# Memory attention on one core: the state update over three engines, logits and scores at other places in a step

## The reference, cut to what matters

```python
x = x + 0.5 * _L0_ffn_ref(_layernorm(x), gate_w, w1, w2)      # 8 experts, top 1
x = x + _L0_attn_ref(_layernorm(x), ...)
x = x + 0.5 * _L0_ffn_ref(_layernorm(x), gate_w, w1, w2)

def _mem_loss(p, k_t, v_t):                 # W1, W2 are 64 x 64
    pred = jax.nn.silu(k_t @ W1.T) @ W2.T
    return jnp.sum((pred - v_t) ** 2)

for c0 in range(0, S, CHUNK):               # CHUNK = 128: 8 chunks
    g = _grad_fn(W_state, k[:, sl], v[:, sl]) * GRAD_SCALE     # per token, norm clipped to 1
    # for each token t: S = eta_t * S - theta_t * g_t;  W = (1 - alpha_t) * W + S
    (S_state, W_state), Wtraj = jax.lax.scan(step, (S_state, W_state), xs)
    h = silu(einsum('btd,btod->bto', q[:, sl], W1t))
    outs.append(einsum('bto,btpo->btp', h, W2t))
out = retrieved @ Wo.T
out = out * rsqrt(mean(out * out, -1) + EPS) * norm_g
return out * (hidden @ gW.T + gb)
```

## Time and profile before

| | |
|---|---|
| median of 3 runs | 743.57 us (742.95 to 744.75) |
| profiled execution, its own time | 744.95 us |
| its span, first to last instruction | 743.1 us |
| busy in it: PE / PEld | 654.3 us (88%) / 574.0 us (77%) |
| busy: DVE / ACT / POOL | 570.0 (77%) / 430.5 (58%) / 249.9 us (34%) |
| attention, roughly | from 195 to 576 us of the span |
| granted TensorE clock, mean | 0.952 |

### The profile page before, as it was taken

One profiled execution on the slowest core, in us unless ns is written; L12 is line 12 of the kernel. 1 busy time (PEld: TensorE's weight loads), 2 busy tenths in 40 slices (PEclk: granted clock), 3 DMA queues, 4 the chain that ended last, 5 costly groups with the idle time before them and its releaser, 6 DMA issues. The chain is left out here.

```text
span 743.1 us, 15272 instructions
## 1 busy us (share of the span) xinstructions
PE 654.3 (88%) x5531; PEld 574.0 (77%) x5531; DVE 570.0 (77%) x1395; ACT 430.5 (58%) x1094; POOL 249.9 (34%) x206
## 2 busy tenths in 40 slices
PE   5538999999697899999999999999988389999995
PEld 2228889898576788989888898988866168999985
DVE  0878888773388989899898989988765878887851
ACT  1416485562355867687786777776643445667450
POOL 0033553123311536162452516243241061651302
PEclk9859999999799999999999999999999579999999
DMA  9959727160332104325141432504123624652401
GB/s 336 413 203 355 275 88 262 51 206 23 128 115 86 59 29 149 110 75 182 58 143 60 140 118 64 195 1 154 48 67 104 227 73 165 238 191 115 141 10 35
DMA packets 63586, 101.97 MB, mean 137 GB/s; under 512 B 8200, under 2 KB 50336, under 8 KB 63392
## 3 DMA queue, kind: packets, MB, share of 16 engines
q1 hardware_dynamic: 51536, 83.01, 32.5%
q0 software_dynamic: 3840, 10.49, 4.3%
q10 hardware_dynamic: 8144, 7.61, 3.3%
HBM read 87.31 MB, written 22.16 MB: 147 GB/s over the span
## 5 line engine op out<-in xcount | busy, mean ns | idle before, releaser
L726 PE MATMUL ps<-moe_normedT_high,weights_high_up 128*128 128x320 f32 x252 | 80.9, 321 | 0.6 <-DVE moe_hidden_low L544 0.5
L727 PE MATMUL ps<-moe_normedT_low,weights_high_up 128*128 128x320 f32 x252 | 78.2, 310 | 0.0
L728 PE MATMUL ps<-moe_normedT_high,weights_low_up 128*128 128x320 f32 x252 | 78.2, 310 | 0.0
L726 PE MATMUL ps<-weights_high_down,moe_hidden_high 128*128 128x256 f32 x256 | 73.5, 287 | 0.3 <-DVE weights_rows L552 0.3
L728 PE MATMUL ps<-weights_high_down,moe_hidden_low 128*128 128x256 f32 x256 | 71.6, 280 | 0.0
L727 PE MATMUL ps<-weights_low_down,moe_hidden_high 128*128 128x256 f32 x256 | 71.5, 279 | 0.0
L544 DVE SCALAR_TENSOR_TENSOR moe_hidden_low<-ps,moe_hidden_high 128x256 fp32r<-128x256 f32 x128 | 53.9, 421 | 22.7 <-ACT moe_hidden_high L681 18.5
L640 ACT CAST weights_high_down<-weights_raw_down 128x256 fp32r<-128x256 f32 x96 | 35.0, 406 | 39.8 <-PE ps L728 33.3
L1247 POOL TENSOR_TENSOR weights_raw_up<-weights_raw_up,att_AB 128x1024 f32<-128x1024 f32 x8 | 17.6, 2197 | 114.0 <-DVE att_ENDS L1457 114.0
L726 PEld LDWEIGHTS ps<-weights_high_down,moe_hidden_high 128*128 128x128 f32 x256 | 48.0, 188 | 3.7 <-issue 3.1
L318 DVE TENSOR_TENSOR weights_low_down<-weights_raw_down,weights_high_down 128x256 fp32r<-128x256 f32 x128 | 49.8, 416 | 0.0
(11 more groups left out here) (326 smaller groups left out, 2008.7 us busy)
## 6 DMA issues: line engine op xcount, KB each, us to landing
weights_raw_up<-in_w SPq DMA_DIRECT2D x16, 1024.0 KB, 7.8
weights_raw_down<-in_w SPq DMA_DIRECT2D x16, 1024.0 KB, 8.2
first_xt<-in_xT SPq DMA_DIRECT2D x8, 1024.0 KB, 8.0
weights_rows<-x SPq DMA_DIRECT2D x8, 1024.0 KB, 5.5
out_x<-weights_rows SPq DMA_DIRECT2D x8, 1024.0 KB, 4.5
weights_rows<-x ACTq DMA_DIRECT2D x7, 1024.0 KB, 5.5
att_AB<-decays_row SPq DMA_DIRECT2D x32, 129.0 KB, 2.9
att_eta<-rates_row SPq DMA_DIRECT2D x8, 512.0 KB, 3.9
```

Source lines behind the costliest of these rows:

```text
L726: mm(dst, high_l, high_r, start=start, stop=False)
L727: mm(dst, high_l, low_r, start=False, stop=False)
L728: return mm(dst, low_l, high_r, start=False, stop=stop)
```

## The change

- The state is made by three engines. ScalarE scales the old state by the decay at the chunk's end into `kept_state` (`scaled_state`, eight activations in two groups). TensorE adds up only the gradients' parts and the momentum's part; MIX shrinks from 128x128 to 64 columns, and its products become 64x64 tiles. VectorE adds both and writes the new state (`new_state`, between two key taps). ScalarE's copies of the sum go.
- `w2_own`, a new tile with W2 of both sides laid out over all partitions, is filled by ScalarE with two copies; the turn of W2 takes four transposes instead of eight.
- The logits of chunk c-1 move: TensorE's products behind the turn of W2, their own turn behind gram, the copies of ScalarE and VectorE ahead likewise.
- Gates 0 and 2 now go to A, 1 and 3 to BB. The scores' products come before the turned keys on TensorE, and P1 before KM on VectorE.
- The decay row gets one more column (a copy on VectorE between the scans). Two constant tiles and one store go.

```diff
     decay, mixed, gain = sb("decay", [B, CH + 1]), ...          # was [B, CH]
+    KM, MIX = sb("KM", [P, B, 2, D]), sb("MIX", [P, B, D])
+    kept_state, w2_own = sb("kept_state", [P, B, P]), sb("w2_own", [P, HALF, P])
...
# SP, spread_decays
-                sp.dma_start(decays_dram[0, :, 0:CH], decay[:]).then_inc(decays_stored, 16)
+                sp.dma_start(decays_dram[0], decay[:]).then_inc(decays_stored, 16)
...
+                    sp.wait_ge(mix_ready, c)
+                    sp.wait_ge(state_scaled, B * c)
...
# GpSimd, mix
-                for n, own, other in SIDES:
-                    g.tensor_tensor(MIX[:, n, own], ...)
-                    g.tensor_tensor(MIX[:, n, other], ...).then_inc(mix_ready, 1)
+                g.tensor_tensor(MIX[:], bc(fold[:].unsqueeze(1), [P, B, D]), bc(AB[:, :, CH - 1:CH], [P, B, D]),
+                                ALU.mult).then_inc(mix_ready, 1)
# GpSimd, setup
+                    g.memset(w2_own[own, :, own], 0.0).then_inc(folded, 1)
...
# VectorE, decay_scans
+                dve.wait_ge(decays_made, 5 * c + 2)
+                v.tensor_copy(decay[:, CH:CH + 1], decay[:, CH - 1:CH]).then_inc(decays_made, 1)
...
# VectorE, gates
-                    src = FIRST_GATES[i] if first_chunk else A if i % 2 else BB
+                    src = FIRST_GATES[i] if first_chunk else BB if i % 2 else A
...
+            def new_state(c, par):
+                dve.wait_ge(state_made, c + 1)
+                dve.wait_ge(state_scaled, B * c + B)
+                v.tensor_tensor(state[1 - par][:, :, D:3 * D], wide(C), kept_state[:], ALU.add).then_inc(state_added, 1)
...
# VectorE, step
                 key_taps(c + 1, 1 - par, range(2, 3))
+                new_state(c, par)
                 second_scores(c, par)
...
                 ends(c + 1, 1 - par, first)
+                if not first:
+                    logits(c - 1)
                 gates(c + 1, 1 - par, (2, 3), first)
+                scores(c + 1)
                 if norm_too:
                     keys(c + 1, 1 - par, False)
                 output_mean(c, 0)
-                if not first:
-                    logits(c - 1)
-                scores(c + 1)
                 key_norms(c + 1, 1 - par)
...
# ScalarE
+            def scaled_state(c, par, batches):
+                act.wait_ge(ab_loaded, 64 * c + 64)
+                if c:
+                    act.wait_ge(state_added, c)
+                for b in batches:
+                    s.activation(kept_state[:, b, :], state[par][:, b, D:3 * D], ACT.Copy,
+                                 scale=AB_ends[:, b, CH:CH + 1]).then_inc(state_scaled, 1)
+
+            def own_w2(st):
+                for n, own, other in SIDES:
+                    last = s.copy(w2_own[own, :, other], st[own, n, 2 * D:3 * D])
+                last.then_inc(w2_own_ready, 1)
+
             def new_state(c, par):
-                act.wait_ge(state_made, c + 1)
-                new = wide(C)
-                s.copy(state[1 - par][:, HALF:B, 0:D], new[:, HALF:B, D:P])
-                s.copy(state[1 - par][:, :, D:3 * D], new).then_inc(state_copied, 1)
+                act.wait_ge(state_added, c + 1)
+                own_w2(state[1 - par])
                 for n, own, _ in SIDES:
-                    last = s.copy(read_w[own, n, 0:D], new[own, n, D:P])
-                last.then_inc(state_copied, 1)
+                    s.copy(read_w[own, n, 0:D], state[1 - par][own, n, 2 * D:3 * D])
# ScalarE, step
+                scaled_state(c, par, range(0, HALF))
                 gradients(c)
...
                 kv_projection(c + 1)
+                scaled_state(c, par, range(HALF, B))
                 q_projection(c + 1, False)
...
                 new_turned(c + 1)
+                if not first:
+                    logits(c - 1)
                 softplus_table()
...
# TensorE
             def gates(c, i):
                 if i == 0:
+                    pe.wait_ge(rates_read, 2 * c + 2)
+                elif i == 1:
                     pe.wait_ge(q_copied, c + 1)
...
-                gate_pair(c, i, A if i % 2 else BB)
+                gate_pair(c, i, BB if i % 2 else A)
             def new_state(c, par):
                 for b in range(B):
-                    mm(dst, MIX[:, b, :], state[par][:, b, D:3 * D], start=True, stop=False, skip_group_check=True)
                     mm(dst[:, 0:D], KM..., grad_w1[:, b, :], start=(b % HALF == 0), ...)
                     mm(dst[:, D:P], hid_m..., grad_w2[:, b, :], ...)
+                for i in range(HALF):
+                    for n, own, other in SIDES:
+                        b = n.start + i
+                        last = mm(wide(C)[own, b, :], MIX[other, b, :], state[par][other, b, D:3 * D], ...)
+            def turn_state(c):
+                pe.wait_ge(w2_own_ready, c + 1)
+                for i in range(HALF):
+                    last = nc.tensor.transpose(wide(C)[:, i, :], w2_own[:, i, :], t["ident"][:])
# TensorE, step
+                turn_state(c + 1)
+                if not first:
+                    logit_products(c - 1)
                 retrieve(c, par)
                 gram(c + 1)
+                if not first:
+                    logit_turn(c - 1)
                 gates(c + 1, 2)
                 outputs(c, 0)
                 gates(c + 1, 3)
+                queries(c + 1, 1 - par)
                 keys(c + 1, 1 - par)
-                if not first:
-                    logit_products(c - 1)
-                queries(c + 1, 1 - par)
-                if not first:
-                    logit_turn(c - 1)
                 hidden(c + 1, 1 - par, False)
```

More of the change, by code:

```diff
@@ L1076, in memory_attention @@
     rates, zeros = sb("rates", [B, 2, CH]), sb("zeros", [B, CH + 1])
-    decay, mixed, gain = sb("decay", [B, CH]), sb("mixed", [B, CH + 1]), sb("gain", [B, CH])
+    decay, mixed, gain = sb("decay", [B, CH + 1]), sb("mixed", [B, CH + 1]), sb("gain", [B, CH])
     theta_log = sb("theta_log", [P, B, D])
@@ L1847, in new_turned @@
                 for n, own, other in SIDES:
-                    last = s.mul(read_w[other, n, D:P], wide(C)[other, n, own], -1.0)
+                    last = s.mul(read_w[other, n, D:P], wide(C)[other, 0:HALF, own], -1.0)
                 last.then_inc(w2_copied, 1)
@@ L1940, in _ @@
             s.copy(idents[:], bc(t["ident"][:].unsqueeze(1), [P, B, CH])).then_inc(folded, 1)
+            act.wait_ge(consts, 16 * len(loads))
+            act.wait_ge(folded, 7)
+            own_w2(state[0])
             first_normalise()
@@ L2157, in new_state @@
                     dst = wide(C)[:, b, :]
-                    mm(dst, MIX[:, b, :], state[par][:, b, D:3 * D], start=True, stop=False, skip_group_check=True)
                     mm(dst[:, 0:D], KM[:, b, :, :].rearrange("p a n -> p (a n)"), grad_w1[:, b, :],
+                       start=(b % HALF == 0), stop=False, skip_group_check=True)
+                    mm(dst[:, D:P], hid_m[:, b, :, :].rearrange("p a n -> p (a n)"), grad_w2[:, b, :],
                        start=False, stop=False, skip_group_check=True)
-                    last = mm(dst[:, D:P], hid_m[:, b, :, :].rearrange("p a n -> p (a n)"), grad_w2[:, b, :],
-                              start=False, stop=True, skip_group_check=True)
+                for i in range(HALF):
+                    for n, own, other in SIDES:
+                        b = n.start + i
+                        last = mm(wide(C)[own, b, :], MIX[other, b, :], state[par][other, b, D:3 * D], start=False,
+                                  stop=True, skip_group_check=True)
                 last.then_inc(state_made, 1)
-            def turn_state(st):
-                for b in range(B):
-                    cols = slice(D, 3 * D) if b < HALF else slice(0, 2 * D)
-                    last = nc.tensor.transpose(wide(C)[:, b, :], st[:, b, cols], t["ident"][:])
+            def turn_state(c):
+                pe.wait_ge(w2_own_ready, c + 1)
+                for i in range(HALF):
+                    last = nc.tensor.transpose(wide(C)[:, i, :], w2_own[:, i, :], t["ident"][:])
                 last.then_inc(state_turned, 1)
@@ L2324, in _ @@
             keys(0, 0, True)
-            queries(0, 0)
+            queries(0, 0, True)
             hidden_turned(0)
```

79 lines of the change are left out of this document (32 added, 47 removed).

## The result

The changed kernel takes 746.45 us (median, 744.5 to 747.12), the kernel before beside it 743.55 us. The ratio is 1.0042, with a 95% interval of 1.0025 to 1.0059: slower by 0.4%. The profiled execution took 746.83 us with a span of 745.0, against 743.1 of before.

What follows compares the result with a forecast made beforehand. TensorE bounds most of a step; at its end TensorE's and ScalarE's chains finish together. Five steps 3.7, plus 0.11, plus 0.57, less 0.75 give +3.6 us: 747.2 against a median of 743.57, range 741.5 to 752.0.

Steps and rivals of the forecast that it cites:

- the tail: From the fourth gate pair done to the next key and value projection: 0.63 us longer, as KM comes later.
- The five steps: Five tails and bodies of attention, each longer by 0.74 us, 3.7 in all.
- step 0: First attention step, without logits: VectorE's reading of the third gate pair holds up the scores; 0.57 us later.
- the prologue: Start of attention: four transposes fewer let the rows be turned sooner; -0.75 us, bounds -0.8 and 0.
- T: Moment in a step when the fourth pair of gates is done on TensorE; the forecast's times count from it.
- K: Moment when the next key and value projection starts on TensorE; forecast 0.63 us later after the fourth gate pair.
- From Silu's start to K 3.47: End of the tail: Silu's start to the next key and value projection stays 3.47 us, 1.28 from the split on.
- The body: From the key and value projection to the fourth gate pair done: -0.72 -0.49 +1.02 +0.3 = +0.11 us a step with logits.
- The rival in which the tiles do not overlap: State update: MIX's tiles take 1.7 us instead of 1.0 in seven steps, +4.5, about 751.7; chance 0.07.
- The meeting of TensorE's arrival at the turn with the state's own chain: Turn of W2: ScalarE's copies end at 392.75, TensorE arrives at 392.9; a faster state gains at most 0.1 us.
- Taken as nothing, bound 0.3 a step: ScalarE's eight scalings of the state in each step: hidden in its waits, so no cost, at most 0.3 us.
- the rival with 0.13: Idle TensorE in the tail lowers the clock: 1 to 1.7 us lost in three to five steps, 751 to 755; chance 0.13.

Runs made afterwards that it cites:

- the first group of experiments: Four edits of the changed kernel: swap undone 0.996; state update alone 0.9941; table load ahead of the squares 1.0021; four unread products a step 1.0062.
- the kernel with KM first: The changed kernel with KM made before P1 on VectorE, TensorE's order unchanged: 764.64 us in one run.

## Why the prediction was right, and where it was not

The time (747.2 forecast, 746.45 measured) and its sign held, and so did the mechanism of the tail: KM behind P1 delays squares, table load and Silu. The terms of the sum held less well. The five steps came 1.07 lower, step 0 1.02 higher, the prologue 0.47 higher, and the end, which had no term, 0.89 lower. That these nearly cancel is luck.

**The tail.** The forecast was +0.63, measured +0.41 (8.53 to 8.94). The links up to Silu came within 0.06 of what I had put: T+5.69 forecast, T+5.63 measured. The step that failed is "The rest is unchanged: from Silu's start to K 3.47". It is 3.30 now. The copies of the turned rows in the kernel before show why (they are not among the rows ahead of the prediction):

```profile
407.34 1.94 PE L1979 MATMUL ps<-ident,weights_rows 128*128 128x128 f32 x16
```

```profile
407.84 0.59 ACT L1804 ACTIVATE att_bend<-ps 128x512 f32<-128x512 f32 x1
408.49 1.02 ACT L1702 CAST att_xT_high<-ps 128x1024 fp32r<-128x1024 f32 x1
409.31 0.37 ACTq L1701 DMA_DIRECT2D weights_rows<-x  x1
409.72 1.01 ACT L1702 CAST att_xT_high<-ps 128x1024 fp32r<-128x1024 f32 x1 [0.21 <-issue]
```

Before, TensorE turned these rows at 407.34, behind `hidden`, the first half was there about 1.0 later, and the first copy started 0.65 after Tanh's start (407.84). Now the rows are turned before Silu, and the copy starts 0.48 after Tanh's start. The other 0.06 is in the links up to Silu. TensorE was in the chain at one more place than I saw, and taking its work away did bring that 0.17. From copy to split (1.05) and from split to K (1.28) nothing moved. The same early turn lets ScalarE issue its DMA before Silu (410.44) instead of between the two copies, where it had cost 0.21; that copy is not on the chain to K.

TensorE's idle time in the tail is 1.92 us, where I had said near 2.4.

**The body.** State update 4.68 forecast, 4.64 measured; the sixteen MIX passes take 1.02 of it, against 1.0. The rival in which the tiles do not overlap (1.7) is out. The Trainium skill, TensorEngine Tiling (Array Packing), section Key Properties, says that tiles of one mode can run in parallel and that changing the mode drains the engine. The 1.02 for sixteen, 0.064 each against 0.112 for a pass of KM or hid_m, is in line with the first but doesn't prove it, since a tile of 64 columns also loads fewer columns and no run here tells the two apart. The second, if it is there, is no more than the 0.1 between the last hid_m products and MIX.

The meeting of TensorE's arrival at the turn with the state's own chain is as forecast, within tenths. The rows on VectorE and ScalarE between the state and the turn (answers to the earlier trace rows):

```profile
437.23 1.21 DVE L1549 TENSOR_TENSOR att_state<-ps,att_kept_state 128x1024 f32<-128x1024 f32 x1
```

```profile
438.47 0.82 ACT L1852 COPY att_w_own<-att_state 64x256 f32<-64x256 f32 x2 [1.91 <-DVE att_state L1549]
```

The copies end at 439.29 and the turn starts at 439.44. In most steps the part from the rates to the turn is 0.77 shorter (forecast 0.72), in two 0.49: there VectorE comes late to the sum of the state, and the row ahead of its scan shows an idle time of 0.27 that ended on nothing the profile shows:

```profile
344.22 0.41 DVE L1433 TENSOR_TENSOR_SCAN att_gain<-att_rates,att_zeros 8x128 f32<-8x128 f32 x1 [0.27 <-issue]
```

That is the step of 0.80 in the table; the other is step 0. From the turn to T it is 0.83 longer, which is 1.02 + 0.3 - 0.49 as forecast. That this sum came out is partly luck. It adds up TensorE's work because "From K to T TensorE is nearly always the last to be ready", and with the state update alone that doesn't hold: its gain of 1.26 is cut by 0.72 at VectorE's gates. The logits' 1.32 happen to fill that 0.72.

**Step 0.** Here the forecast was +0.57 and it is +1.59. In the tail 0.76 (8.17 to 8.93) stands for 0.57. The rest, 0.83, is what the prediction has as "Taken as nothing, bound 0.3 a step": the scalings. In step 0 ScalarE is the last engine, for it has the logarithms there between two table loads:

```profile
238.00 1.28 ACT L1847 ACTIVATE att_kept_state<-weights_raw_up,att_AB 128x128 f32<-128x128 f32 x4
...
244.86 1.01 ACT L1730 COPY att_raw_kv<-ps 128x1024 f32<-128x1024 f32 x1
```

```profile
245.93 0.50 PE L2005 MATMUL ps<-att_xT_high,att_w_high 128*128 128x512 f32 x1 [1.63 <-ACT att_raw_kv L1730]
```

Between the four scalings (1.17 to the next start) and the copy ScalarE never stands idle. The copy of the keys and values is at 244.86, 17.51 after the first T, and was at 244.05, 16.42 after it: 1.09 later, which is 1.17 for the scalings, 0.21 for a later first copy of the rows, less 0.28 since the second follows sooner. TensorE waits 1.63 for the bank instead of 0.73. With the scalings moved, 0.84 of the step comes back. In the other steps they do lie in waits; there the forecast of nothing held.

**Prologue and end.** The rows are turned 0.64 earlier (201.20 for 201.84), and of that 0.28 reach the first T. The forecast of -0.75 took it that TensorE's turn is all that the first T hangs on. One pair of profiles can't settle this term: in the four kernels of the first group of experiments, with the same prologue as the kernel after, the first T lies between 225.87 and 226.59, and in the kernel after at 227.35. At the end I had no term, and 0.89 was gained behind the last T, 0.28 of it by the turn of the hidden layer (6.29 to 6.01). It goes with the logits, whose products now lie ahead of that T: in the profiles with no fall in the last step it is 31.71 to 31.94 to the turn of chunk 6's logits with the logits moved, and 32.61 to 32.74 with them in the old place.

**The clock.** In its own profile the kernel after has a granted clock of 1.00 in steps 1 to 6 (the first window above is one of them), and the rival with 0.13 did not happen. Only step 0 has a fall, the one behind the prologue's wait, which the kernel before has too. Its premise is real, though. In the kernel with KM first and in the one with twice the squares the clock fell in one of the six usual steps. The stretch before the fall and the fall itself, of each:

```profile
501.00:505.00 4.00, 2.44 (x31) 2.04 (x28) 2.71 (x6) 3.21 (x6) 0.98 (x2) 1.00 0.00 0
505.10:508.50 3.40, 3.40 (x18) 3.40 (x17) 2.67 (x6) 2.69 (x5) 1.56 (x2) 0.50 0.03 7
```

```profile
508.50:512.50 4.00, 1.90 (x16) 1.41 (x14) 2.25 (x5) 3.97 (x8) 1.49 (x2) 1.00 0.00 0
512.50:515.90 3.40, 3.40 (x13) 2.24 (x12) 3.03 (x5) 3.36 (x11) 1.80 (x1) 0.50 0.00 0
```

TensorE was busy for 2.44 and 1.90 of the 4.00 us ahead. T to K of these steps is 9.82 instead of 8.82, and 10.03 instead of 9.49, and the steps take 44.90 instead of 43.97 and 45.68 instead of 44.60, so a fall costs 0.9 to 1.1 here. Why one step of several with the same pattern falls stays open.

It was not tried whether the squares could run before or beside KM; both read the keys' bank.

## What to carry to other kernels

Where two engines' chains end a stretch together, shortening one shows nothing, and a reordering that helps it may feed the other later: follow the products to be read first through every engine until the next projection. A change of several parts is worth taking apart even when its sum is near zero: here the state update alone gained 0.6%, with the logits moved as well 0.4% was left, and the swap took that and more. An operation hidden in waits in the usual step must be placed anew in the first, where another engine may be last.

## What the runs showed of the hardware

One wait of TensorE of 2.43 us in the prologue was followed by a granted clock of 0.50 for 0, 3.4, 6.8 or 10.2 us, also among kernels whose instructions are the same up to there, and that made one step 43.65 to 47.6 us long. With eleven unread products in its place the clock was 1.00 behind it in five profiles of five, and they were worth 0.3% to the kernel before.

What a fall of 3.4 us costs depends on its place: 1.5 us right behind the first T (45.13 against 43.67), 0.9 to 1.1 in the tail of a usual step, 1.1 at the end of the attention, and nothing at 10.6 us after the first T. It comes in some executions and not in others, so a single profile of such a kernel can carry up to 4 us in one step, and 1.1 at the end, that are no part of the change.
